# Later edge stages of a graph network: one operand of the one-hot comparisons in PSUM, the third stage on both partition halves, two matmuls taken in turn

## What is computed

```python
edge_index = jnp.stack([src, dst])
# layer 1
msg = jax.nn.relu(x[src] + edge_attr @ We + be)
aggr = jax.ops.segment_sum(msg, dst, num_segments=x.shape[0])
# layer 2
he = _mlp(edge_z, edge_ln_w, edge_ln_b, edge_W, edge_b)        # 64 -> 32
msg = jnp.concatenate([hn[src], he], axis=-1)                   # 32 + 32
emb_edge = _mlp(msg, red_ln_w, red_ln_b, red_W, red_b)          # 64 -> 64
msg_sum = jax.ops.segment_sum(emb_edge, dst, num_segments=n_nodes) + emb_local
# layer 3 (six heads)
s = jax.nn.leaky_relu(gl[src] + gr[dst], NEG_SLOPE)
e = jnp.einsum('ehf,hf->eh', s, att)
p = jnp.exp(e - m[dst])
alpha = p / (denom[dst] + 1e-16)
msg = alpha[:, :, None] * gl[src]
out = jax.ops.segment_sum(msg, dst, num_segments=n)
```

## Time and profile before

| | |
|---|---|
| median of 3 runs | 5894.8 us (5892.7 to 5896.9) |
| profiled execution | 5869.05 us, of it 5867.1 us span |
| PE busy | 4853.4 us (83%) |
| DVE busy | 3834.0 us (65%) |
| ACT busy | 2429.3 us (41%) |
| POOL busy | 4041.6 us (69%) |
| edge0 / edge1 / edge2 / edge3a / edge3b, about | 1450 / 1110 / 1116 / 1069 / 615 us |

### The profile page before, as it was taken

How to read it: one execution, slowest core, us unless ns; L and a number is a source line. 1 busy time by engine, 2 the same in 40 slices (tenths; PEclk the granted TensorE clock), 3 DMA queues, 4 the chain that set the end, 5 groups by cost and what they waited for, 6 DMA issues and landing times. The chain is left out here.

```text
span 5867.1 us, 96832 instructions
## 1 busy us (share of the span) xinstructions
PE 4853.4 (83%) x27328; PEld 3591.7 (61%) x27328; DVE 3834.0 (65%) x6280; ACT 2429.3 (41%) x6303; POOL 4041.6 (69%) x3386
## 2 busy tenths in 40 slices
PE   4999999999678777884888888859999999159997
PEld 3454555544466666663777777756666666049996
DVE  5787777777322222225566666658887888889997
ACT  2999889888200000000444444421111111037774
POOL 4888888887377777760777777747777777147774
PEclk7999999999665556555777787869999999579998
DMA  3333333333111111120111111124444445111111
GB/s 87 78 81 76 80 76 77 81 74 62 24 38 38 38 38 38 38 32 3 40 36 37 36 38 38 38 41 129 131 133 126 130 132 127 26 45 48 47 49 33
DMA packets 482309, 369.52 MB, mean 63 GB/s; under 512 B 354912, under 2 KB 377889, under 8 KB 482265
## 3 DMA queue, kind: packets, MB, share of 16 engines
q1 hardware_dynamic: 371363, 269.65, 16.2%
q0 software_dynamic: 104448, 94.21, 10.1%
q10 hardware_dynamic: 6454, 5.13, 0.3%
HBM read 333.06 MB, written 35.55 MB: 63 GB/s over the span
## 5 line engine op out<-in xcount | busy, mean ns | idle before, releaser
L793 POOL DMA_INDIRECT edge_src_rows<-table_wh,edge_gather_idx x816 | 1118.7, 1371 | 263.1 <-issue 260.7
L689 POOL DMA_INDIRECT edge_src_rows<-table_h,edge_gather_idx x816 | 817.4, 1002 | 348.7 <-issue 251.0
L689 POOL DMA_INDIRECT edge_cat<-table_hn,edge_gather_idx x816 | 830.9, 1018 | 278.9 <-issue 248.9
L689 POOL DMA_INDIRECT edge3a_src_rows<-table_h,edge3a_gather_idx x816 | 786.6, 964 | 320.4 <-issue 256.1
L821 PE MATMUL edge_sums_ps<-edge_onehot_src,edge_halves 128*128 128x512 bf16 (+1 forms) x4284 | 888.6, 358 | 95.4 <-DVE edge_onehot_src L893 95.4
L1055 DVE TENSOR_TENSOR layers_accT<-layers_accT,edge_sums_ps 64x128 f32 (+1 forms) x1632 | 360.7, 280 | 911.0 <-PE edge_sums_ps L1114 441.6
L821 PEld LDWEIGHTS edge_sums_ps<-edge_onehot_src,edge_halves 128*128 128x128 f16 x4284 | 388.8, 100 | 530.8 <-DVE edge_onehot_src L893 101.8
L893 DVE TENSOR_SCALAR edge_onehot_src<-layer_node_row,edge_src_col,edge_magnitude 128x3136 bf16<-128x3136 f16 x612 | 672.6, 1100 | 2.0 <-PE edge_sums_ps L821 2.0
L860 ACT ACTIVATE edge_onehot_src_act<-edge_distance,edge_magnitude,edge_minus_magnitude 128x3136 bf16<-128x3136 f16 x204 | 612.2, 3001 | 10.4
L855 ACT ACTIVATE edge_distance<-layer_node_row,edge_src_col 128x3136 f16<-128x3136 f16 x204 | 591.9, 2901 | 2.8 <-ACT edge_onehot_src_act L860 0.4
L1417 PE MATMUL edge3a_z_ps<-Wz,edge3a_both_ends_t 128*128 128x396 f32 x1632 | 583.0, 511 | 1.5 <-ACT edge3a_both_ends_t L1452 1.1
(11 more groups left out here) (288 smaller groups left out, 8116.7 us busy)
## 6 DMA issues: line engine op xcount, KB each, us to landing
edge_dst_row<-in_dst_row SPq DMA_DIRECT2D x102, 512.0 KB, 3.8
edge3a_dst_row<-in_dst_row SPq DMA_DIRECT2D x102, 512.0 KB
edge_window<-table_wh SPq DMA_DIRECT2D x816, 32.5 KB
edge_edge_attr<-in_ea SPq DMA_DIRECT2D x102, 256.0 KB
edge3a_window<-table_h SPq DMA_DIRECT2D x816, 32.0 KB
kept_rows<-edge3a_src_rows SPq DMA_DIRECT2D x102, 256.0 KB, 2.4
edge3b_src_rows<-kept_rows SPq DMA_DIRECT2D x102, 256.0 KB
edge_src_rows<-table_wh,edge_gather_idx POOLq DMA_INDIRECT x816
```

Source lines behind the costliest of these rows:

```text
L689: nc.gpsimd.indirect_dma_start(self.slot(h, j), None, self.table[:, :], bass.IndirectOffsetOnAxis(ap=self.idx[h][:, j:j + 1], axis=0)).the ...
L793: nc.gpsimd.indirect_dma_start(g[q][:, j, :], None, k.t_wh[:, :], bass.IndirectOffsetOnAxis(ap=idx[q][:, j:j + 1], axis=0)).then_inc(gathe ...
```

## The change

Three things change, in edge1, edge2, edge3a and edge3b; edge0 and the node stages stay.

1. **A PSUM operand for the comparisons.** At its start a stage copies `k.row0` into PSUM once, and `onehot` compares `k.dst_rel` (SBUF) with that copy. In edge3a the eight node numbers of a batch are copied from `k.win_node` into PSUM by a new short step `nodes`, once a batch, between the first and the second weighing of the batch before the last, and `onehot_t` compares `drow` with them. In edge2 `ec` and `rc` are copied into PSUM too, so the additions at lines 1289 and 1302 have one SBUF operand. The comparison takes the shape [P, B, 1, P].
2. **edge2 on both partition halves.** `ea`, `catTp` and `catT` become 128 x 4 x 128: tile i lies on partitions 0 to 63 and tile 4 + i on 64 to 127. The eight transposes become four of 128 x 128, ACT's copy of `catTp` goes from 64 x 1024 to 128 x 512, and the matmuls for `hep` and `rp` alternate between the lower and the upper 64 partitions. `eR` and `rR` are held on both halves. The edge attributes are laid out to match, so the DMA has the same bytes on twice the partitions. The last step of `edge_row` becomes two instructions of half the size. The gather writes to other places of `cat`.
3. **edge3a's two row matmuls alternate.** `turn` waits for the gather at once, and then runs the window's matmul and the source's matmul tile by tile.

```diff
@@ setup
-                pe.matmul(fold[0:D, 0:HALF], k.center[:, :], k.eWw[:, :], start=True, stop=True)
...
+                for o in (0, D):
+                    pe.matmul(fold[o:o + D, 0:HALF], k.center[:, :], k.eWw[:, :], start=True, stop=True)
...
-def onehot(dve, k, out, t, h):
-
-    return dve.tensor_tensor(out, over(k.dst_rel[:, bass.ds(t * 2 * B + h * B, B)], P),
-                             rows_over(k.row0[:, :], B), ALU.is_equal)
+def onehot(dve, k, out, t, h, row):
+
+    a = row.shape[1]
+    own = k.dst_rel[:, bass.ds(t * 2 * B + h * B, B)].unsqueeze(2).unsqueeze(3)
+    return dve.tensor_tensor(out.rearrange("p b (a w) -> p b a w", a=a), own.to_broadcast([P, B, a, P // a]),
+                             row.unsqueeze(1).to_broadcast([P, B, a, P // a]), ALU.is_equal)
...
@@ edge1 (edge3b alike)
+        row = c.ps("columns_ps", [P, 1, P])
+                dve.tensor_copy(row[:, 0, :], k.row0[:, :]).then_inc(row_ready, 1)
+                dve.wait_ge(row_ready, 1)
-                            onehot(dve, k, oh[1 - h][:, :, :], t + h, 1 - h).then_inc(oh_ready, 1)
+                            onehot(dve, k, oh[1 - h][:, :, :], t + h, 1 - h, row[:, :, :]).then_inc(oh_ready, 1)
...
@@ edge2
-        catT = c.sb("cat_t", [D, ROWS])
+        catT = c.sb("cat_t", [P, B // 2, P])
-        catTp = c.ps("cat_t_ps", [D, ROWS])
+        catTp = c.ps("cat_t_ps", [P, B // 2, P])
+        fixed = c.ps("constants_ps", [P, 512])
+        row, ec, rc = fixed[:, 0:P].unsqueeze(1), fixed[:, P:P + HALF], fixed[:, 2 * P:2 * P + D]
...
-                    for j in range(B):
-                        mm = pe.matmul(hep[:, j, 0:HALF + D], ea[h][:, j * P:(j + 1) * P], k.eR[:, :],
-                                       start=True, stop=True)
+                    for i in range(B // 2):
+                        for a in (0, 1):
+                            half = slice(a * D, (a + 1) * D)
+                            mm = pe.matmul(hep[:, 4 * a + i, 0:HALF + D], ea[h][half, i, :], k.eR[half, :],
+                                           start=True, stop=True)
...
+                        for i in range(B // 2):
+                            mm = pe.transpose(catTp[:, i, :], cat[h][:, i, :, :].rearrange("p a d -> p (a d)"),
+                                              k.ident[:, :])
...
-                    dve.tensor_tensor(he2[:, :, :], he[:, :, :], rows_over(k.ec[:, :], B),
+                    dve.tensor_tensor(he2[:, :, :], he[:, :, :], rows_over(ec, B),
                                       ALU.add).then_inc(he_b, 1)
...
-                    dve.tensor_tensor(u2[:, :, :], u[:, :, :], rows_over(k.rc[:, :], B),
+                    dve.tensor_tensor(u2[:, :, :], u[:, :, :], rows_over(rc, B),
                                       ALU.add).then_inc(u_b, 1)
...
@@ edge3a
+        nums = c.ps("window_nodes_ps", [P, 2, B])
                     pe.wait_ge(win_ready[h], B * 16 * tt)
+                    pe.wait_ge(ga.gathered[h], B * 16 * tt)
                     for j in range(B):
                         cols = slice(j * P, (j + 1) * P)
                         pe.matmul(hcTp[D:P, cols], win[h][:, j, :], oht[h][:, cols], start=True, stop=True)
-                    pe.wait_ge(ga.gathered[h], B * 16 * tt)
-                    for j in range(B):
-                        cols = slice(j * P, (j + 1) * P)
                         mm = pe.matmul(hcTp[0:D, cols], g[h][:, j, :], k.ident[:, :], start=True, stop=True)
...
+                def nodes(n, h, t):
+                    dve.wait_ge(oht_ready, n)
+                    dve.tensor_copy(nums[:, h, :], k.win_node[:, bass.ds(t * 2 * B + h * B, B)]
+                                    ).then_inc(nums_ready, 1)
...
                     dve.tensor_tensor(tiles3(oht[h][:, :]), tiles3(drow[h][:, :]),
-                                      over(k.win_node[:, bass.ds(t * 2 * B + h * B, B)], P),
+                                      over(nums[:, h, :], P),
                                       ALU.is_equal).then_inc(oht_ready, 1)
```

76 lines of the change are left out of this document (48 added, 28 removed).

## The result

| | us |
|---|---|
| before, median of 4 runs | 5895.85 (5892.72 to 5901.13) |
| after, median of 4 runs | 5752.54 (5750.39 to 5757.71) |
| ratio | 0.9759 (0.9743 to 0.9774) |
| profiled execution before / after | 5869.05 / 5753.16 |

The changed kernel is 143 us faster, 2.4%. The forecast was 99 us, 5796 with a range of 5772 to 5860: right in direction and in mechanism, too small by 44 us, and outside the range. Between the two profiled executions the difference is 115.9 us; the other 27 us lie between the profiled execution of before and its median.

The account below looks back on a forecast made before the run. POOL, full with 816 gather instructions a stage, was taken to bound edge1, edge2 and edge3a (PE edge3b). 42.6 + 43 + 15.5 - 2 = 99 us off the median 5894.8 gave 5796 us, range 5772 to 5860.

Parts of the forecast that it names:

- POOL paces edge1, edge2 and edge3a, and a longer gather instruction lengthens the stage one for one: edge1, edge2, edge3a: POOL is full with 816 gather instructions a stage, a floor of 1015 us each.
- Two tensors in SBUF hold the gather, one in PSUM does not: Gather instructions starting inside a DVE instruction with two SBUF tensors run long; beside one PSUM tensor they take 0.94 us.
- Edge1, 42.6 us: edge1: gain from the comparison's PSUM operand, all long gather instructions gone but one of 5.38 us at the start.
- Edge2, 43 us: edge2: gain from comparison and both constants in PSUM; 17 us of extra gather time remain in lines 1305 and 1292.
- Edge3a, 15.5 us: edge3a: gain from the comparison's PSUM operand, all the extra gather time in line 1490 gone.
- the lower bound of 5777: Whole kernel: the forecast's own fastest time, 5796 - 17 - 2, with edge2's remaining 17 us gained too.
- Additions, 2 us: Stage starts: seven small copies cost 0 to 3 us, taken as 2; other added DVE work falls in idle time.
- the turn, 0: edge3a: the window's matmuls moved behind PE's wait for the gather cost 0, since POOL needs no late engine.
- The comparison keeps 1.22 us, edge3b is unchanged: DVE's comparison costs the same with a PSUM operand, 1.22 us; edge3b, where PE is busy 607 of 615 us, stays.
- No effect of the operand: Rival: the PSUM operand frees no gather instruction; 5897 us, chance 0.05.
- The slow change of half: Rival, edge3a and edge2: each change of half costs PE 0.16 us, 224 and 100 us lost; 6120 us, chance 0.05.
- The fall of PE's clock: Rival, edge3a: longer PE waits lower its granted clock; halfway, at 0.68, 153 us lost, 5949 us; chance 0.08.

Follow-up runs that it names:

- relu_in_psum: Changed kernel with the last step of edge2's message split into two instructions, the half-way result in PSUM; 5788.75 us, ratio 0.9811.
- the two spare comparisons: Changed kernel plus an unread second comparison per batch in edge1, in two versions: operand in PSUM 5759.85 us, operand in SBUF 5793.86 us.
- rest_only: Changed kernel with comparison and addition operands back in SBUF, keeping halves, turn order and edge3a's small copy; 5885.43 us, ratio 0.9971.
- edge3a_only: Kernel before with only the node numbers of edge3a's comparison copied into PSUM; 5854.69 us, ratio 0.9918.
- edge3a_sbuf: Kernel before with edge3a's node numbers copied into an SBUF tile instead of PSUM; 5891.25 us, ratio 0.9988.
- old_turn: Changed kernel with edge3a's window matmuls again before the gather wait and the source's eight behind it; 5760.01 us, ratio 0.9759.
- spare_sbuf: Changed kernel plus an unread second comparison per batch in edge1 with both tensors in SBUF; 5793.86 us, ratio 0.9825.
- before_fourth: Kernel before, unchanged, in a further profiled execution; 5909.86 us, one run.
- psum_1_3a_3b: Kernel before with the comparison's operand in PSUM in edge1, edge3a and edge3b, edge2 untouched; 5805.07 us, ratio 0.9838.

## Why the prediction was right in kind and wrong in size

**POOL paces edge1, edge2 and edge3a, and a longer gather instruction lengthens the stage one for one**: right. Lengths of the stages and surpluses fell together (47.6 and 47.5, 46.9 and 47.8, 16.6 and 16.7), and the sum above holds for thirteen executions within 5 us. What can end this is a loop that grows past POOL's lap, and `relu_in_psum` shows that case.

**Two tensors in SBUF hold the gather, one in PSUM does not**: right, by the two spare comparisons, 34 us against 0.

**Edge1, 42.6 us**: measured 47.5 in the trace, 49.6 by runs. The 5.38 us instruction at the stage's start, which I had let stand because it lay behind a memset, went as well. The rows of before say more of it:

```profile
1545.35 2.83 DVE L1136 MEMSET layers_accT<- 65x3328 f32 x1 [0.64 <-issue]
1545.82 5.38 POOL L689 DMA_INDIRECT edge_src_rows<-table_h,edge_gather_idx  x1 [0.30 <-issue]
1548.10 2.29 DVE L709 TENSOR_TENSOR edge_onehot<-dst_rel,row 128x1024 f32<-128x1024 f32 x2
```

It ends 0.81 us after the end of the two comparisons that follow the memset (1548.10 + 2.29 to 1545.82 + 5.38), as the others end behind theirs. So it seems to have been held by them and not by the memset, though it started 2.28 us ahead of them. It is not the operand alone that took it away: in `rest_only`, where the new small copy stands between memset and comparisons but the operand is in SBUF, a gather instruction that starts inside the memset takes 0.94 us, and none of edge1 exceeds 2.02. Why an instruction that started so early could be held is open.

**Edge2, 43 us**: 47.8 in the trace, of operand and halves together. The residue is 12.8 us and not 17, in the two lines that were named, and within the bounds for it.

**Edge3a, 15.5 us: the step that failed.** The median of timed runs gave 47.4. The 15.5 was read correctly from the profiled execution, and was then subtracted from a median 26 us above that execution, with the sentence that the gain is of instructions counted in it. That sentence hid the question where the 26 us came from. They were the same thing: in the other three profiled executions of before, edge3a's surplus is 26 to 42 us higher, and the rest of the span moves by 5 us at the most. So the change removes them too: 143.3 = 26.8 (5895.85 less 5869.05) + 115.9 (between the profiled executions) + 0.6. What the traces show is four executions; that the 26 us of the timed runs are the same is inferred from those and from `edge3a_only`, which gains 47.4 and whose timed runs scatter over 11 us, where those of `edge3a_sbuf` scatter over 44.

The range had the same fault. It let edge2's residue move, since DVE meets POOL at other moments, and did not let the surplus **of before** move for that same reason. The rows had the warning: in the profiled execution a gather instruction started 0.93 us into the comparison and was held 0.16 us, and a start at the middle would have cost 0.5. 102 batches at 0.5 us are 51 us for edge3a, 35.5 more than the 15.5, and the lower bound of 5777 less these, some 5741, would have held the result.

**Additions, 2 us, and the turn, 0**: the turn cost 0 (`old_turn`). The additions don't show: beyond the gathers the span is 3.7 us shorter, of which 2.9 lie between edge2's last gather and edge3a's first. Of the 17 us by which the profiled difference (115.9) exceeds my 99, 11 are in the three surpluses and 6 in these.

**The comparison keeps 1.22 us, edge3b is unchanged**: right, 1.21 us; PE 605.5 of 615 us. On POOL one thing did change there that I had not looked at: the product beside the comparison got shorter, and PE hid it (below).

**The rivals.** No effect of the operand: excluded. The slow change of half: the pairs follow at 0.11 to 0.12 us, excluded. The Trainium skill (TensorEngine Tiling (Array Packing), Key Properties), by which different tiles multiply in parallel, agrees: 32 MATMULs take 1.97 us where a block of 16 took 1.96. The fall of PE's clock: I had given it 0.08, and it would have eaten the gain from 0.71 down; PE waits 2.0 us a batch in edge3a (2.2 by the working), and the granted clock of the stretch goes from 0.99 to 0.96 only, near the upper of its two levels (2.4 GHz). The long wait in a stage does not by itself bring the 0.59 of edge1.

The Trainium skill (SBUF — State Buffer, Who interferes with whom) states both rules that I had weighed. Its rule that a DVE instruction with two SBUF inputs contends with a GpSimd instruction that reads SBUF agrees with edge1, edge2 and edge3a of every run here, but for the 5.38 us above, and so does its rule that one with at most one, outside the two-port modes, does not. Its inference that a `tensor_tensor` leaves a DMA issued by GpSimd alone is contradicted for these indirect DMAs by the 1.58 us above and the 34 us of `spare_sbuf`.

## What to carry to other kernels

Before you subtract a gain read in one profiled execution from a median, ask what the difference between that execution and the median consists of; if the change removes the very cost that varies, it removes the varying part too. Where GpSimd's DMA issue sets the pace, look for the gather instructions above the shortest duration and at the operands of the DVE instruction in which each starts; a constant operand in PSUM cost one small copy here and nothing per use. In edge0 even the median is held (below). Engine time that is freed beside the pacing engine (162 us of PE in `old_turn` against after) is worth nothing until the pace changes.

## What of the hardware was not expected

**In edge1, edge2 and edge3a a held gather instruction ends 0.81 us after the DVE instruction that holds it, wherever in it it started.** In the rows above it ends 0.81 us after the end of the comparison (4303.51 + 1.22 to 4303.78 + 1.76) and again (4313.97 + 1.22 to 4314.60 + 1.41); in the earlier trace rows 0.81, in the earlier trace rows 0.81, and in the earlier trace rows behind line 1305's 0.69 us 0.81. Of the 193 gather instructions of edge1, edge2 and edge3a in before's profiled execution that start in the first 1.05 us of a comparison with two SBUF tensors, those between the 5% and the 95% point end 2.03 to 2.04 us after its start; in `before_fourth`, with 260 such, it is 2.03 to 2.05. So a hit costs the holder's duration less the offset less 0.13 us. Five of the 193 are not held: they start in the first 0.04 us of the comparison and take 0.94 us, and there the comparison takes 1.26 to 1.30 us instead of 1.22. The waiting of one is paid by the whole stage, and its size depends on a phase of tenths of a microsecond. The timed runs of before lie between 5872 and 5917 us and those of after between 5750 and 5761; that the phase accounts for all of the difference in spread is inferred.

**The product on GpSimd is slowed by the comparison as well.** In edge3b POOL's product of 1920 elements, which reads two SBUF tensors, takes 3.47 us instead of 4.33 (441.3 / 102) now that the comparison beside it reads PSUM. In `psum_1_3a_3b` it takes 3.47 as well, and in `rest_only`, with the comparison back on SBUF, 4.33, so it is the operand. The row of after:

```profile
L1721 POOL TENSOR_TENSOR edge3b_weighted<-edge3b_src_rows,edge3b_alpha 128x1920 f32<-128x1920 f32 x102 | 353.6, 3467 | 260.3 <-DVE edge3b_alpha L1813 249.4
```

That is 88 us less of POOL's time, in a stage that PE bounds; where POOL's product bounds a stage, the same edit should shorten it, which was not tried.

**Two SBUF tensors are not the only thing that holds a gather instruction.** edge0, which the change leaves alone, shows it in the page and the timeline of after:

```profile
L798 POOL DMA_INDIRECT edge_src_rows<-table_wh,edge_gather_idx x816 | 1116.3, 1368 | 263.0 <-issue 260.6
807.04 1.11 DVE L898 TENSOR_SCALAR edge_onehot_src<-layer_node_row,edge_src_col,edge_magnitude 128x3136 bf16<-128x3136 f16 x1
807.66 1.79 POOL L798 DMA_INDIRECT edge_src_rows<-table_wh,edge_gather_idx  x1 [0.30 <-issue]
```

Line 898 reads one large SBUF tensor and two numbers for each partition. All 289 gather instructions that start inside it take 1.13 us or more, and their surplus is 204 of edge0's 346 us (1116.3 less 770.3). POOL waits for nothing else there either, 1376 us from the first to the last of them. So the largest surplus of this kernel was never in the change. What taking it away would bring is open: PE is busy 1327 and ACT 1255 us of 1440 in that stage.
